# Pacing the mixing-weight loads on GpSimd's queue, and the store of the second half of the mixed coefficients, in a four-layer spectral network

## What is computed

```
h = layer_norm(x @ fc0_w + fc0_b)                      # 32 channels
for i in range(4):
    w1, w2 = w1r[i] + 1j*w1i[i], w2r[i] + 1j*w2i[i]    # mixing weights, 32 x 32 x 12 x 12 each
    x_ft = rfft2(h)                                    # only 24 x 12 frequencies are used
    out_ft[:, :, :12, :12]  = einsum('bixy,ioxy->boxy', x_ft[:, :, :12, :12], w1)
    out_ft[:, :, -12:, :12] = einsum('bixy,ioxy->boxy', x_ft[:, :, -12:, :12], w2)
    h = layer_norm(irfft2(out_ft) + conv1x1(h, conv_w[i]) + conv_b[i])
    if i < 3: h = gelu(h)
h = gelu(h @ fc1_w + fc1_b); h = gelu(h @ fc2_w + fc2_b); h = h @ fc3_w + fc3_b
```

## Time and profile before

| | us |
|---|---|
| Time before, median of 3 runs | 3339.99 |
| Lowest and highest of the 3 | 3336.26, 3341.17 |
| The profiled execution's own time | 3339.68 |
| Its span in the trace | 3337.9 |

### The profile page before, as it was taken

How to read it: one execution, slowest core, us unless ns; L and a number is a source line. 1 busy time by engine, 2 the same in 40 slices (tenths; PEclk the granted TensorE clock), 3 DMA queues, 4 the chain that set the end, 5 groups by cost and what they waited for, 6 DMA issues and landing times.

```text
span 3337.9 us, 82078 instructions
## 1 busy us (share of the span) xinstructions
PE 2942.9 (88%) x32240; PEld 1869.3 (56%) x32240; DVE 2146.3 (64%) x3954; ACT 1948.7 (58%) x2271; POOL 61.5 (2%) x81
## 2 busy tenths in 40 slices
PE   5888888999888999888999879999999987973994
PEld 2454555666555666565666644444444447962893
DVE  5888676888666888666888745444544444246457
ACT  4777655666545666455666547777777763422451
POOL 0000000000000000000000010000000001000000
PEclk9999999999999999999999999999999998986897
DMA  4222346444437444447444524111111000000000
GB/s 107 99 95 98 99 161 205 163 163 162 154 135 207 162 162 162 151 144 210 163 162 162 163 75 101 55 46 44 57 54 57 29 1 1 1 1 0 1 1 13
DMA packets 98092, 335.90 MB, mean 101 GB/s; under 512 B 29928, under 2 KB 61960, under 8 KB 62088
## 3 DMA queue, kind: packets, MB, share of 16 engines
q1 hardware_dynamic: 93832, 295.73, 25.7%
q0 software_dynamic: 4096, 37.75, 4.9%
HBM read 179.29 MB, written 154.14 MB: 100 GB/s over the span
## 4 chain that ended last, share of the span: by engine, by line
PE 75%; DVE 11%; issue 5%; ACT 5%; DMA 4%; SPq 0%; DVEq 0%; POOL 0%; ACTq 0%; POOLq 0%
PE pA L1281 14%; PE pA L1289 7%; PE pT L1375 7%; PE pS L1318 4%; PE pT L1307 4%; PE pD L1364 4%; PE pD L1332 4%; PE pD L1346 4%; PE pD L467 3%; PE pA L467 3%; PE pA L1271 3%; PE pD L1253 2%; DMA y_in<-y_scratch 2%; PE pS L459 2%; PE pT L459 2%
## 5 line engine op out<-in xcount | busy, mean ns | idle before, releaser
L1610 DVE TENSOR_REDUCE small<-arena 128x32 f32<-128x1056 f32 x320 | 396.8, 1240 | 322.5 <-ACT arena L1451 314.0
L1281 PEld LDWEIGHTS pA<-conv_bd,h_in 128*128 128x128 f32 x4096 | 479.8, 193 | 109.4 <-issue 92.7
L1281 PE MATMUL pA<-conv_bd,h_in 128*128 128x128 f32 x4096 | 518.1, 280 | 8.6 <-DVE arena L1603 2.9
L1441 ACT COPY w_sb<-pA 128x1024 f32<-128x1024 f32 x256 | 259.7, 1015 | 417.3 <-PE pA L1289 346.4
L1624 DVE SCALAR_TENSOR_TENSOR w_sb<-w_sb,small 128x1024 f32<-128x1024 f32 x320 | 386.6, 1212 | 5.5
L1462 ACT ACTIVATE h_new<-pT,bet,gam 128x1024 f32<-128x1024 f32 x256 | 307.4, 1201 | 126.6 <-PE pT L1307 121.1
L1451 ACT ACTIVATE arena<-w_sb 128x1024 f32<-128x1024 f32 x320 | 339.2, 1060 | 13.4
L1307 PEld LDWEIGHTS pT<-cst,w_sb 128*128 128x128 f32 x2048 | 225.5, 143 | 142.8 <-issue 124.4
L1307 PE MATMUL pT<-cst,w_sb 128*128 128x128 f32 x2048 | 283.3, 282 | 21.4 <-DVE w_sb L1624 21.1
L1466 ACT COPY h_rows<-pS 128x1024 f32<-128x1024 f32 x256 | 257.0, 1004 | 72.2 <-PE pS L1318 72.1
L1318 PEld LDWEIGHTS pS<-cst,h_new 128*128 128x128 f32 x2048 | 229.4, 143 | 113.4 <-issue 72.8
(11 more groups left out here) (299 smaller groups left out, 3921.2 us busy)
## 6 DMA issues: line engine op xcount, KB each, us to landing
h_scratch<-h_new SPq DMA_DIRECT2D x128, 1024.0 KB, 4.2
h_in<-h_scratch SPq DMA_DIRECT2D x128, 1024.0 KB, 5.0
y_scratch<-w_sb POOLq DMA_DIRECT2D x32, 576.0 KB, 8.4
y_in<-y_scratch SPq DMA_DIRECT2D x512, 36.0 KB
w_sb<-in_L_tok_w1r_dram POOLq DMA_DIRECT2D x8, 576.0 KB, 16.6
w_sb<-in_L_tok_w1i_dram POOLq DMA_DIRECT2D x8, 576.0 KB, 16.6
w_sb<-in_L_tok_w2r_dram POOLq DMA_DIRECT2D x8, 576.0 KB, 21.0
w_sb<-in_L_tok_w2i_dram POOLq DMA_DIRECT2D x8, 576.0 KB, 21.0
```

The lines of the kernel that those rows point to most:

```text
L1281: pe.matmul(pA[:, c:c + 128], h_in[:, 1024 * n + c:1024 * n + c + 128], conv_bd[:], start=(j == 0), stop=False, skip_group_check=True)
L1441: act.copy(raw[n], pA[:]).then_inc(s["copied"], 1)
L1610: dve.reduce_sum(var[n], sq[n % 2], axis=AX).then_inc(s["summed"], 1)
```

## The change

The 8 weight DMAs of a layer are issued as four pairs (slot 0 w1, slot 0 w2, slot 1 w1, slot 1 w2), and POOL waits before them for counts of acc_full, the accumulations that PE has finished. In phase "first" the pairs wait for the first accumulation of groups 0, 1, 3 and 4. In a mid phase the first pair waits for mix half 1 to be read out, the second for the second accumulation of group 2, then `y_store(L, 1)` waits for the first accumulation of group 4, and the last two pairs for the first accumulations of groups 5 and 6. The semaphore w_loaded is split by slot: `cen.0` waits for its own slot's four DMAs, in each iteration, with one more increment of a counter on DVE. On SP the wait `y_is_stored(L, 1)` (in phase "first": `mlp_params`) moves from behind group 1 to behind group 5, and groups 1 to 5 become a loop. Layer 3's `y_store(L, 1)` stays where it was.

```diff
--- before.py
+++ after.py
@@ -357,7 +357,7 @@
...
-                 "turned", "h_new_ok", "x_loaded", "y_loaded", "y_clear", "packed", "h_loaded0", "h_loaded1", "stored0", "stored1", "fc0_clear", "y_stored", "w_loaded",
+                 "turned", "h_new_ok", "x_loaded", "y_loaded", "y_clear", "packed", "h_loaded0", "h_loaded1", "stored0", "stored1", "fc0_clear", "y_stored", "w_loaded0", "w_loaded1",
...
@@ -1094,12 +1094,13 @@
 
             def groups(ph, L):
 
-                group(ph, L, 1)
+                with sp.Fori(1, 6) as g:
+                    group(ph, L, g)
                 if ph == "mid":
                     y_is_stored(L, 1)
                 else:
                     mlp_params()
-                with sp.Fori(2, NG - 1) as g:
+                with sp.Fori(6, NG - 1) as g:
                     group(ph, L, g)
                 group(ph, L, NG - 1)
 
@@ -1126,13 +1127,16 @@
             pool.memset(arena[:, 7744:8384], 0.0).then_inc(s["conv_cleared"], 1)
             pool.memset(mlp, 0.0).then_inc(s["mlp_cleared"], 1)
 
-            def weights(L):
-                for slot in range(2):
-                    for w, (wr, wi) in enumerate((("L0_tok_w1r", "L0_tok_w1i"), ("L0_tok_w2r", "L0_tok_w2i"))):
-                        for r in range(2):
-                            q = slice(64 * w + 32 * r, 64 * w + 32 * r + 32)
-                            pool.dma_start(w_v[q, slot].rearrange("p o m -> p (o m)"),
-                                           ins[wr if slot == r else wi][L].rearrange("i o x y -> i (o x y)")).then_inc(s["w_loaded"], 16)
+            def weights(L, slot, w):
+                wr, wi = (("L0_tok_w1r", "L0_tok_w1i"), ("L0_tok_w2r", "L0_tok_w2i"))[w]
+                for r in range(2):
+                    q = slice(64 * w + 32 * r, 64 * w + 32 * r + 32)
+                    pool.dma_start(w_v[q, slot].rearrange("p o m -> p (o m)"),
+                                   ins[wr if slot == r else wi][L].rearrange("i o x y -> i (o x y)")).then_inc(s[f"w_loaded{slot}"], 16)
+
+            def after(ph, L, g, n):
+
+                pool.wait_ge(s["acc_full"], at("acc", ph, L, g, n))
 
             def y_store(L, half):
 
@@ -1147,7 +1151,10 @@
                         src = w_sb[q:q + 32, 13312:17920].rearrange("b (w n) -> b w n", w=2)
                         pool.dma_start(dst, src).then_inc(s["y_stored"], 16)
 
-            weights(0)
+            for slot in range(2):
+                for w in range(2):
+                    after("first", 0, 3 * slot + w, 1)
+                    weights(0, slot, w)
             for L in range(LAYERS):
                 y_store(L, 0)
                 if L == 0:
@@ -1155,9 +1162,20 @@
                 else:
                     pool.wait_ge(s["acc_full"], at("acc", "mid", L, 0, 0))
                 pool.tensor_copy(conv_bd[:], conv_all[:, P * L:P * L + P]).then_inc(s["conv_ready"], 1)
-                y_store(L, 1)
-                if L < LAYERS - 1:
-                    weights(L + 1)
+                if L == LAYERS - 1:
+                    y_store(L, 1)
+                else:
+                    n = 2 * L + 1
+                    pool.wait_ge(s["mix_a_free"], 3 * n + 3)
+                    pool.wait_ge(s["mix_b_free"], 3 * n + 3)
+                    weights(L + 1, 0, 0)
+                    after("mid", L, 2, 2)
+                    weights(L + 1, 0, 1)
+                    after("mid", L, 4, 1)
+                    y_store(L, 1)
+                    for w in range(2):
+                        after("mid", L, 5 + w, 1)
+                        weights(L + 1, 1, w)
             pool.wait_ge(s["mix_a_full"], 6 * LAYERS)
             pool.wait_ge(s["mix_b_full"], 6 * LAYERS)
             pool.memset(spec[:, 0:at_col[0]], 0.0).then_inc(s["par_cleared"], 1)
@@ -1577,8 +1595,9 @@
                 L, i, part = centring["L"], centring["i"], centring["part"]
                 w = w_v[:, part, :, bass.ds(24 * i, 24)]
                 first = 18 * part + n
-                if n == 0 and part == 0:
-                    dve.wait_ge(s["w_loaded"], 128 * L + 128)
+                if n == 0:
+                    dve.wait_ge(s[f"w_loaded{part}"], 64 * L + 64)
+                    alone(dve)
                 dve.wait_ge(s["w_centred"], 36 * L + first + 1 + 3 * i)
                 alone(dve)
                 if n == 0:
```

## The result

| | before | after |
|---|---|---|
| Median of 4 runs, us | 3338.55 | 3284.55 |
| Lowest and highest | 3336.26, 3341.17 | 3281.69, 3286.36 |
| Profiled execution's own time | 3339.68 | 3281.69 |
| Its span | 3337.9 | 3279.5 |

The ratio is 0.9837, with a 95% interval of 0.982 to 0.9854: 54 us faster, where 3284 us was forecast.

The account below looks back on a forecast made before the run. It took late small loads behind POOL's DMAs to bound the kernel: fc0 at the start, y_in in three mid phases. 3339.68 - 15.4 - 40.4 = 3283.9, said as 3284 us; 8-in-10 range 3275 to 3308.

Parts of the forecast that it names:

- The start: Program start: with no weights in flight, fc0 loads land at about 13.4 instead of 28.87, gaining 15.4 us.
- The SP wait and y_in: Body 3 of mid phases: y_in, issued from about 512.7, lands by 522 to 525, so wait and low clock go.
- The size of the mid phases' gain: Three mid phases: 43.9 us lost, less 1.5 for low clock and 2 for overlong body 2, gains 40.4 us.
- body 2's excess: Body 2 of mid phases, ahead of the y_in wait: 8.5 us too long, of which 2 kept, bounds 0 and 8.5.
- The second pair and cen.0: Body 3, DVE: second pair lands about 525, cen.0 stands at 535.4; cost 0, bound 15.4 us.
- Body 4: Body taking the late store: 22.1 of 27.65 us DMA work, y_in lands at about 22; cost 0 us.
- The software queue's price: POOL's DMA queue: one DMA costs 2.36 us of all engines.
- mlp_params: Phase "first", SP: moves past four x loads; 13 issues hold one x load back by 7 us; cost 0 to 1 us.
- A: Mid phases: body 3's y_in or the second pair still late by some 4 us each, 21 us, time 3305; chance 0.13.
- B: Program start: doesn't gain, time 3299; chance 0.07.
- C: Mid phases: second pair lands in 35.7 us, stopping DVE 15.4 us; 55 us, time 3339, no change; chance 0.06.
- D: Mid phases: all overlength of body 2 and low clock after the mix go as well, 3279 or below; chance 0.04.

Follow-up runs that it names:

- start undone: Changed kernel with layer 0's eight weight loads at the very start again, rest of the change kept: 3302.49 us, ratio to before 0.9884.
- store undone: Changed kernel with the store of half 1 straight behind mix half 1 and SP's wait behind group 1, weights still in pairs: 3297.50 us, ratio to before 0.9867.
- pairs undone: Changed kernel with all eight weight loads of a layer straight behind mix half 1, store and SP's wait still late: 3293.24 us, ratio to before 0.9852.
- store twice: Changed kernel with the late store's four 576 KB transfers issued once more into an unread scratch in each mid phase: 3314.51 us, ratio to before 0.9925.
- start alone: Changed kernel with the mid phases as before, only layer 0's weight loads paced: 3320.42 us, ratio to before 0.9932.

## Why the prediction was right, step by step

**The start: right, a little small.** The term was 15.4 us, with the landing of 2.3 us taken from rows 10. The loads were there 1.0 us after the last issue (12.09 - 11.11), so it is 16.8. The undone start confirms it: 3302.49 against 3284.55 is 17.9 us in the medians.

**The SP wait and y_in: right.** No wait for y_in is left, body 3 runs at the full clock, and the DMA share of body 2 is 0.81 where I had said about 0.8. The cause was right as well, and the experiments sharpen it: neither the early store nor the burst alone, but the sum of work in front of y_in. The same sum, from the shares of the two queues, put y_in 0 to 3 us late for the store undone and the pairs undone (measured: none, and at most 2.0), and about 5 us late for the store twice (measured: 8.3).

**The size of the mid phases' gain: 2.9 us too large.** From body 2 to body 4 the changed kernel takes 541.45 - 486.27 = 55.18 us in L=0, 1027.39 - 968.16 = 59.23 in L=1 and 1510.48 - 1452.59 = 57.89 in L=2, after 69.20, 70.68 and 69.91: 14.0 + 11.5 + 12.0 = 37.5 us for the 40.4 of the sum. The term at fault is what I kept of body 2's excess: 2 us, plus 1.5 for the low clock in L=2, where 6.4 are left. The instruction gaps shrank (3.60 to 0.55), but the low clock came in L=1 too, where the kernel before had opened at 0.91 us, and body 2 there is 3.94 us too long. The same code taken a second time has the low clock in L=0 and L=1 and not in L=2, and the start undone, with the same mid phases, not in L=1, so I do not put it down to the change. Outside the start and the three stretches the span lost 58.4 - 16.8 - 37.5 = 4.1 us that no step of mine had: 1.2 and 1.0 between the mid phases and 2.1 behind the last one. What made them isn't shown. Errors of 1.4 and 4.1 us one way and 2.9 the other leave 2.6 us of the span. That 3284 lies within 0.6 us of the median is luck on top: the profiled execution, in which the spans above are read, was the fastest of its four, 2.9 us below their median.

**The second pair and cen.0: right.** I had reckoned about 10 us to landing; it takes at most 9.3 in L=0, 8.6 in L=1 and 10.7 in L=2, and DVE has no wait for the weights.

**Body 4: right, with less room than it seemed.** I had y_in landed 22 us into the body, its issue ended 564.77 - 541.45 = 23.3 us into it. What I had not foreseen is that SP itself is held while it issues: 13.27 us for the 4.55 of the sum. The software queue's price was also low: the row for the changed kernel between 486 and 514 (packets, MB, share of 16 engines) is

```profile
q0 software_dynamic: 192, 2.36, 39.5%
```

so four loads take 0.395 x 28 = 11.1 us of all engines, 2.8 each, for the 2.36 I had from rows 7. The row corrects the packets too: a pair has 96 and not 128, 6 for each engine. The Trainium skill's rule of turns, packet by packet ("DMA: Bandwidth & Descriptors", "Queues, rings and completion order"), isn't told apart from my reckoning by these runs: where y_in has more small pieces than POOL has large ones, both say that it ends with the last large one.

**mlp_params: right.** The x load behind it goes out at 172.35, and the next transposes of x start at 176.58, without a wait:

```profile
172.35 0.39 SPq L973 DMA_DIRECT2D h_in<-in_x_dram  x1
```

**The rivals.** A (late again in the new place) did not occur, and the store twice shows it 2.36 MB away, with 8.3 us of waiting in each phase where rival A had 4. B (no gain at the start) is ruled out by the start alone, whose interval ends at 0.9957. C (the second pair late) did not occur, nor did D: body 2's excess stayed in part. Nothing was slower.

## What to carry to other kernels

A wait for a small load can be a wait for everything that was queued on the DMA engines before it. Add up that work from the shares of the queues, and compare it with the time to the next use, body by body. Move bulk transfers that are due much later into bodies whose DMA share is low, and check that the small load of that body still has room. Where two batches together make a stall, each may look innocent when it is put back alone. And take a second profile of the same kernel before you explain a few microseconds: here it moved both the low clock and the gap in PE's instructions.

## What the runs showed of the hardware

- **PE can stand still for its instructions.** The gap at one place of body 2 was up to 4.66 us. In all 14 gaps over 0.2 us PE went on 1.3 to 1.7 us after the end of a 16 KB packet of the instruction queue. With the burst or the early store beside it, the gaps of the three phases add up to 5.11, 6.79, 6.19 and 2.50 us (kernel before, start alone, store undone, pairs undone); with the changed kernel's order to 0.55 and 1.88 us in its two profiles, 0 in the start undone. That the crowd on the DMA engines is what holds the packet back is my inference from this difference; the sizes don't follow the load one by one.
- **SP's issuing can be held up by POOL's transfers.** Eight y_in issues took 4.65 us in body 2 of the changed kernel, 13.27 beside the store in body 4, and 20.56 beside two stores. A high DMA load alone doesn't do it: in the kernel before they took 4.11 us at a DMA share of 0.96, and in the pairs undone, 5.9 us after the last of the eight weight issues, 3.79. What makes the difference is open.

```profile
495.47 3.79 SPq L996 DMA_DIRECT2D y_in<-y_scratch  x8
```

- **Small loads land quickly on idle DMA engines.** The 17 loads of the first projection were there 1.0 us after the last issue, and 17.7 us after it beside 4.7 MB of POOL's.
- **The low clock after a mix comes and goes.** The same program had body 2 of L=0 at 27.53 us in one profile and at 29.43 in the other, where it opened at the low clock. Its nine runs on record go from 3281.69 to 3292.15 us, so a change of 5 us can't be told from single runs; how much of this spread is the clock isn't shown.
